# A fused attention and expert kernel: the row scores run six steps ahead of the column scores instead of eight

## The chip, the cores and the metric

The kernel runs on one core of one Trainium2 chip. The metric is the device time of one execution in microseconds (us). A TensorE clock of 1.00 in the profile is the full 2.4 GHz, 0.50 is 1.2 GHz. Engines are named as the profile names them: PE is TensorE, DVE is VectorE, ACT is ScalarE, POOL is GpSimd, SP is SyncE, which issues most DMAs here.

## The reference, cut to what matters

```
x: 16 batches x 512 tokens x 256 features, 16 heads of 16
n = layernorm(x)
Q, K, V = n Wq^T + bq, n Wk^T + bk, n Wv^T + bv          (per head)
scores  = Q K^T / 4 + lambda * (tanh(Q) J) tanh(K)^T      (causal: j > i gives -inf)
x = x + softmax(scores) V Wo^T + bo
x = x + swiglu_shared(layernorm(x)) + sum over the top 2 of 8 experts, each weighted
```

The change touches only the attention stage, which is a little over half of the time. The routing and the experts after it are the same before and after.

## The kernel before, in words

Attention works on one batch at a time, in 16 steps of one batch (`STEPS`). Four groups of four heads make four steps each: step n handles head group n // 4 and the key tile jt = n % 4 of 128 keys. Because of the causal mask, the scores of that step are (4 - jt) * 128 wide: 512, 384, 256, 128 columns in the four steps of a group.

Each score is computed twice. The **columns** (keys on the partitions, queries along the free axis, `ps_cols`, L532 and L536) are what the softmax uses. ACT takes their exponential (L623), POOL zeroes the masked corner (L801), and PE multiplies with V (`pv`, L554) one step later. The exponential must have each row's maximum taken off. The maximum comes from the **rows** (queries on the partitions, `ps_rows`, L525), which PE computes LEAD steps ahead: DVE adds the mask and takes the maximum in one instruction per head (L680, followed by a short read of the accumulator into `mx`). When the four row tiles of a head group are done, DVE writes the negated maxima as two parts into `nm` (L689, L691). PE turns them with four transposes into `ps_m` (the piece `"mt"`, L463), ACT copies them to `mT` (L610), and the matmul of L536 adds them to the columns. The first columns of a group wait for this copy.

A step is made of two halves, s = 0 and s = 1. In a half PE issues two heads of rows and the two other heads of columns, four matmuls side by side in the array, and then L536 for these columns. There are three PSUM banks for rows and three for columns. So a half can be issued only when DVE has finished the first maximum of the half before, and ACT the first exponential of the half before. After half 0 comes the "piece" with place 0, after half 1 `pv` of the step before and the piece with place 1. In `PIECES` an entry is (step, place, kind, index, batch relative to the one whose columns run). Pieces are the projections and the other small products: `xt` transposes of the normalized input, `k`, `q`, `qj`, `v` projections of the next batch, `mt` turned maxima, `out` output projection, `gt` and `lg` the router's part of the batch before. All pieces use one PSUM bank, `ps_m`, and each waits until the engine that empties it has taken the piece before (`taken`).

DVE's order in a step is: maxima of half 0, its part of piece 0, maxima of half 1 and, at the end of a head group, the two instructions on `nm`, then piece 1. After that follow, at some steps, small jobs: `invert` (n = 1 and 9), `normalize` (L731, n = 5 and 13), `layer_norm` of the input of the batch after next (L667, n = 9), `statistics` (n = 11 to 14).

With LEAD = 8 and tiles numbered from the widest down, the rows of step n are just as wide as its columns, and a group of rows begins at a step with n % 4 = 0 and ends at n % 4 = 3. Before batch 0 there is a prologue of 16 steps without columns: the projections of batch 0, then, from step 8 on, eight steps of rows alone, with six banks (`first_rows`), among which DVE takes the statistics of the later inputs (L755). In the last batch the rows end at step 7, and eight steps of columns alone follow.

The k and q data go through SP's DMAs into `ks` and `qs`, and the first rows of a batch (step 8 of the batch before) wait for them. All instructions are unrolled; there is no loop register.

Of the kernel before, what the change touches and what calls it, by code (L numbers as in the profile page):

```python
# [34 lines left out]
TT = S // P  # L35
NT = NB * TT
HG = 4
# [7 lines left out]
NSLOT = 2 * NT + NE - 1  # L45
ZR = 3
EARLY = 4
LEAD = 8
STEPS = G * TT
STRIP = 2 * HD  # L50
PART_PAIRS = ((0, 0), (0, 1), (1, 0))
# [29 lines left out]
def over_batches(eng, batch):  # L81
# [7 lines left out]

PIECES = [  # L90
    (0, 0, "xt", 0, 1), (0, 1, "xt", 1, 1),
    (1, 0, "mt", 1, 0),
    (2, 0, "k", 0, 1),
    (3, 0, "k", 1, 1),
    (4, 0, "q", 0, 1),
    (5, 0, "q", 1, 1), (5, 1, "mt", 2, 0),
    (6, 0, "qj", 0, 1),
    (7, 0, "qj", 1, 1),
    (8, 0, "v", 0, 1),
    (9, 0, "v", 1, 1), (9, 1, "mt", 3, 0),  # L100
    (10, 0, "out", 0, -1),
    (11, 0, "out", 1, -1),
    (12, 0, "gt", 0, -1),
    (13, 0, "gt", 1, -1),
    (14, 0, "mt", 0, 1),
    (15, 0, "lg", 0, -1),
]
PER_BATCH = {"xt": 2, "k": 2, "q": 2, "qj": 2, "v": 2, "mt": G, "out": 2, "gt": 2, "lg": 1}
# [67 lines left out]
def attention_stage(nc, ctx, sbt, x_v, wqT, bq, wkT, bk, wvT, bv, woT, bo, J, lam,  # L176
# [213 lines left out]
    def count(kind, j, b):  # L390

        return b.v * PER_BATCH[kind] + j + 1

    def unit(b, n):

        m = n + LEAD
        return b.plus(m // STEPS), (m % STEPS) // TT, TT - 1 - m % TT

    def row_no(g, it, h):

        return (g * TT + TT - 1 - it) * HG + h

    def col_no(n, s, e):

        return n * HG + 2 * s + e

    def bank_of(u):

        return 1 if u == STEPS * HG - 1 else u % 3

    def first_rows(d, u):

        return d.off == 0 and u < STEPS * HG // 2

    def row_bank(d, u):

        return (*ps_rows, *ps_cols)[u % 6] if first_rows(d, u) else ps_rows[bank_of(u)]

    def last_use(u):

        w = u - 1
        while bank_of(w % (STEPS * HG)) != bank_of(u):
            w -= 1
        return w
# [4 lines left out]
    def _(pe):  # L429
# [55 lines left out]
        def half(b, n, s):  # L485

            HEADS = STEPS * HG
            d, g, it = unit(b, n)
            gc, jt = n // TT, n % TT
            has_rows = d.at_least(0) and d.at_most(NB - 1)  # L490
            has_cols = b.at_least(0) and b.at_most(NB - 1)
            if has_rows and first_rows(d, row_no(g, it, 0)):
                if s == 1:
                    return
                if g == 0 and it == TT - 1:
                    for loaded in (k_in, q_in):
                        pe.wait_ge(loaded[0], 64)
                if row_no(g, it, 3) >= 6:
                    pe.wait_ge(max_done, row_no(g, it, 3) - 5)
                for h in range(HG):  # L500
                    at = STRIP * h
                    mm = nc.tensor.matmul(row_bank(d, row_no(g, it, h))[:, 0:(it + 1) * P],
                                          qs[at:at + STRIP, d.par, g, it * P:(it + 1) * P],
                                          ks[at:at + STRIP, d.par, g, 0:(it + 1) * P], start=True, stop=True)
                    if h % 2:
                        mm.then_inc(rows_ready, 1)
                return
            if has_rows:
                if g % 2 == 0 and it == TT - 1 and s == 0:
                    for loaded in (k_in, q_in):  # L510
                        pe.wait_ge(loaded[g // 2], (d.v + 1) * 64)
                w = max(last_use(row_no(g, it, 2 * s + e)) for e in range(2))
                if w >= 0 or d.at_least(1):
                    pe.wait_ge(max_done, d.v * HEADS + w + 1)
            if has_cols:
                if s == 0 and jt == 0:
                    pe.wait_ge(taken["mt"], count("mt", gc, b))
                w = max(last_use(col_no(n, s, e)) for e in range(2))
                if w >= 0 or b.at_least(1):
                    pe.wait_ge(exp_done, b.v * HEADS + w + 1)  # L520
            if has_rows:
                for e in range(2):
                    h = 2 * s + e
                    at = STRIP * h
                    mm = nc.tensor.matmul(ps_rows[bank_of(row_no(g, it, h))][:, 0:(it + 1) * P],  # L525
                                          qs[at:at + STRIP, d.par, g, it * P:(it + 1) * P],
                                          ks[at:at + STRIP, d.par, g, 0:(it + 1) * P], start=True, stop=True)
                mm.then_inc(rows_ready, 1)
            if has_cols:
                for e in range(2):  # L530
                    at = STRIP * (2 * (1 - s) + e)
                    nc.tensor.matmul(ps_cols[bank_of(col_no(n, s, e))][:, jt * P:S], ks[at:at + STRIP, b.par, gc, jt * P:(jt + 1) * P],  # L532
                                     qs[at:at + STRIP, b.par, gc, jt * P:S], start=True, stop=False)
                for e in range(2):
                    at = STRIP * (2 * (1 - s) + e)
                    mm = nc.tensor.matmul(ps_cols[bank_of(col_no(n, s, e))][:, jt * P:S], ones_r[at:at + STRIP],  # L536
                                          mT[at:at + STRIP, gc % 2, jt * P:S], start=False, stop=True)
                mm.then_inc(cols_ready, 1)
# [19 lines left out]
        def batch(b):  # L558
            att = b.at_least(0) and b.at_most(NB - 1)
            for n in range(STEPS):  # L560
                if b.fixed and b.off == PROLOGUE and n == 8:
                    pe.wait_ge(const_ready, 2)
                half(b, n, 0)
                piece(b, n, 0)
                half(b, n, 1)
                if n > 0 and att:
                    pv(b, n - 1)
                if n == 0 and b.at_least(1):
                    pv(b.plus(-1), STEPS - 1)
                if b.off == TAIL and n == 0:  # L570
                    pe.wait_ge(max_done, NB * STEPS * HG)
                    fill(ps_rows[0], 42)
                if b.off == TAIL and 10 <= n < 15:
                    fill(ps_rows[0], 3)
                piece(b, n, 1)
# [81 lines left out]
    def _(dve):  # L657
# [12 lines left out]
        def maximum(b, n, s):  # L670
            d, g, it = unit(b, n)
            if not (d.at_least(0) and d.at_most(NB - 1)):
                return
            gb = g % 2
            dve.wait_ge(rows_ready, d.v * (STEPS * 2) + row_no(g, it, 2 * s) // 2 + 1)
            dve.nop(nofuse=True)
            for e in range(2):
                h = 2 * s + e
                bank = row_bank(d, row_no(g, it, h))[:, 0:(it + 1) * P]
                nc.vector.tensor_tensor_reduce(out=bank, in0=bank, in1=maskrow[:, (TT - 1 - it) * P:S], scale=1.0,  # L680
                                               scalar=LOWEST, op0=ALU.add, op1=ALU.max, accum_out=mx[:, gb, it, h:h + 1])\
                    .then_inc(max_done, 1)
            if it == 0 and s == 1:

                dve.wait_ge(max_done, d.v * (STEPS * HG) + (g + 1) * TT * HG)
                if g > 0 or d.at_least(1):
                    dve.wait_ge(ready["mt"], d.v * G + g)
                pair = nm[:].rearrange("p t (h c) -> p t h c", c=STRIP)
                nc.vector.tensor_scalar(pair[:, :, :, 0], mx[:, gb], -1.0, None, ALU.mult).then_inc(nmh_ready, 1)  # L689
                dve.wait_ge(nmh_ready, d.v * G + g + 1)  # L690
                nc.vector.scalar_tensor_tensor(out=pair[:, :, :, 1], in0=mx[:, gb], scalar=-1.0,  # L691
                                               in1=pair[:, :, :, 0].bitcast(F32), op0=ALU.mult, op1=ALU.subtract)\
                    .then_inc(nm_ready, 1)
# [1135 lines left out]
```

## Time and profile before

| | |
|---|---|
| time, median of 3 runs | 2139.71 us (2135.65 to 2140.8) |
| profiled execution, its own time | 2137.79 us |
| its span, first to last instruction | 2136.1 us |
| PE, DVE, ACT, POOL busy | 92%, 58%, 50%, 38% of the span |
| prologue, rows alone | 57.99 to 87.19 us |
| batches with columns | 87.19 to 1147 us |

A timeline row of the profile gives the start in us, the duration in us, the engine, the source line, the operation, output and inputs, and how many instructions were merged; in brackets stands how long the engine was idle before and what ended that.

### The profile page before, as it was taken

How to read it: one execution, taken by the hardware profiler on the slowest of the kernel's cores; microseconds unless marked ns; L12 is line 12 of the kernel's file. 1: busy time of each engine (PE TensorE's matmuls, PEld its weight loads, DVE VectorE, ACT ScalarE, POOL GpSimd, SP SyncE). 2: the span in 40 equal slices, each digit the busy share in tenths (PEclk: the TensorE clock that was granted, in tenths of full speed). 3: DMA queues.
4: the chain of work that ended last, by engine and by line, in shares of the span. 5: the costliest groups of instructions: out<-in, count | busy, mean ns of one | idle time of the engine just before them, and what ended most of it. 6: DMA issues, size and time to landing. Idle time of an engine off the chain costs nothing. (4 is left out here: it accounts for less than half of the span.)

```text
span 2136.1 us, 48445 instructions
## 1 busy us (share of the span) xinstructions
PE 1957.2 (92%) x14755; PEld 1296.5 (61%) x14824; DVE 1246.5 (58%) x3875; ACT 1065.7 (50%) x2310; POOL 820.6 (38%) x1206
## 2 busy tenths in 40 slices
PE   2689999999999999999988999997999999999997
PEld 1345445454454544545435788886777777777776
DVE  5666667766667666776662865553445545444553
ACT  1255555555555555555552345452555555555553
POOL 4033323333323333233332037773444444444443
PEclk9799999999999999999999999999999999999999
DMA  7234443344443434434322346654863333333332
GB/s 240 60 106 117 121 136 124 110 118 119 136 130 107 122 111 140 128 114 124 100 87 79 137 134 226 223 188 150 215 167 58 57 55 55 56 55 57 54 57 34
DMA packets 156641, 246.08 MB, mean 115 GB/s; under 512 B 29408, under 2 KB 90592, under 8 KB 156480
## 3 DMA queue, kind: packets, MB, share of 16 engines
q1 hardware_dynamic: 120960, 189.24, 28.9%
q0 software_dynamic: 32064, 53.44, 12.2%
q8 instruction: 91, 1.49, 0.3%
q10 hardware_dynamic: 3456, 1.34, 0.3%
q14 instruction: 70, 0.57, 0.1%
HBM read 111.89 MB, written 90.50 MB: 95 GB/s over the span
## 5 line engine op out<-in xcount | busy, mean ns | idle before, releaser
L680 DVE CUSTOM_DVE_ANT_0 ps_rows<-ps_rows,maskrow 128x128 f32<-128x128 f32 (+1 forms) x1009 | 477.1, 514 | 290.9 <-PE ps_rows L525 282.2
L623 ACT ACTIVATE probs<-ps_cols 128x512 f32<-128x512 f32 (+3 forms) x1024 | 392.0, 435 | 386.7 <-PE ps_cols L536 380.1
L525 PE MATMUL ps_rows<-ks,qs 32*128 32x512 f32 x1984 | 403.1, 480 | 73.5 <-DVE mx L680 38.6
L532 PE MATMUL ps_cols<-qs,ks 32*128 32x512 f32 (+3 forms) x2048 | 418.5, 485 | 2.5 <-ACT probs L623 2.4
L1642 POOL DMA_INDIRECT out_dram<-y_e,to x135 | 216.1, 1601 | 349.4 <-DMA out_dram<-y_e,to 221.5
L799 POOL TENSOR_TENSOR pace<-eps 1x1 f32<-1x1 f32 x256 | 58.2, 227 | 747.0 <-ACT probs L623 747.0
L525 PEld LDWEIGHTS ps_rows<-ks,qs 32*128 32x128 f32 x1984 | 153.3, 184 | 268.5 <-DVE mx L680 221.9
L536 PE MATMUL ps_cols<-mT,ones_r 32*128 32x512 f32 (+3 forms) x1024 | 284.8, 550 | 0.0
L1771 DVE TENSOR_TENSOR h_lo<-ps_h,h_hi 128x512 fp32r<-128x512 f32 x135 | 93.3, 691 | 232.6 <-ACT h_hi L1746 232.6
L1740 ACT ACTIVATE sg_e<-ps_ge 128x512 f32<-128x512 f32 x135 | 80.7, 598 | 263.1 <-PE ps_ge L1664 261.0
L554 PE MATMUL ps_o<-probs,vt 128*32 128x512 f32 (+3 forms) x2048 | 192.5, 448 | 0.8 <-POOL probs L801 0.8
L1407 POOL DMA_INDIRECT xs_d<-row,pos x128 | 131.3, 1026 | 134.2 <-issue 118.5
L532 PEld LDWEIGHTS ps_cols<-qs,ks 32*128 32x128 f32 x2048 | 154.8, 185 | 9.7 <-ACT probs L623 7.6
L801 POOL TENSOR_SCALAR_AFFINE_SELECT probs<-probs 128x512 f32<-128x512 f32 x256 | 159.8, 624 | 0.0
L680 DVE DVE_READ_ACCUMULATOR2_ANT mx<- 128x1 f32 x1024 | 144.4, 141 | 0.1
L1787 DVE TENSOR_TENSOR h_e<-sg_e,ps_ue 128x512 f32<-128x512 f32 x135 | 92.9, 688 | 71.1 <-PE ps_ue L1664 71.1
L1633 POOL DMA_DIRECT2D xr<-xs_d x133 | 127.6, 959 | 14.8 <-DVE to L1796 14.1
L536 PEld LDWEIGHTS ps_cols<-mT,ones_r 32*128 32x128 f32 x1024 | 99.5, 188 | 51.3 <-issue 31.5
L1664 PE MATMUL ps_ge<-w_hi,x_lo 128*128 x270 | 111.4, 493 | 0.0
L1664 PE MATMUL ps_ue<-w_hi,x_lo 128*128 x270 | 109.2, 485 | 0.0
L1080 PE MATMUL ps_g<-x2T,swg 128*128 128x512 f32 x384 | 99.8, 396 | 1.4 <-DVE x2T L1190 1.4
L1133 ACT ACTIVATE sg<-ps_g 128x512 f32<-128x512 f32 x64 | 37.9, 593 | 126.6 <-PE ps_g L1080 94.6
(220 smaller groups left out, 3838.9 us busy)
## 6 DMA issues: line engine op xcount, KB each, us to landing
xs_d<-zrows SPq DMA_DIRECT2D x45, 408.0 KB, 2.9
xr<-xs_d POOLq DMA_DIRECT2D x135, 136.0 KB, 3.3
whi_d<-w_sh SPq DMA_DIRECT2D x16, 768.0 KB, 3.8
w_hi<-whi_d SPq DMA_DIRECT2D x24, 512.0 KB
xn<-in_L_attn_x_dram SPq DMA_DIRECT2D x16, 512.0 KB, 5.2
ks<-k_lin SPq DMA_DIRECT2D x64, 128.0 KB, 3.0
ks<-k_tan SPq DMA_DIRECT2D x64, 128.0 KB, 3.7
qs<-q_lin SPq DMA_DIRECT2D x64, 128.0 KB, 2.4
```

Source lines behind the costliest of these rows:

```text
L525: mm = nc.tensor.matmul(ps_rows[bank_of(row_no(g, it, h))][:, 0:(it + 1) * P], qs[at:at + STRIP, d.par, g, it * P:(it + 1) * P], ks[at:at ...
L532: nc.tensor.matmul(ps_cols[bank_of(col_no(n, s, e))][:, jt * P:S], ks[at:at + STRIP, b.par, gc, jt * P:(jt + 1) * P], qs[at:at + STRIP, b. ...
L536: mm = nc.tensor.matmul(ps_cols[bank_of(col_no(n, s, e))][:, jt * P:S], ones_r[at:at + STRIP], mT[at:at + STRIP, gc % 2, jt * P:S], start= ...
L554: mm = nc.tensor.matmul(ps_o[2 * HD * h:2 * HD * (h + 1), jt * P:S], vt[:, b.par, jt, g * HG + h], probs[:, n % 2, h, jt * P:S], start=jt ...
L623: nc.scalar.activation(probs[:, n % 2, 2 * (1 - s) + e, jt * P:S], ps_cols[bank_of(col_no(n, s, e))][:, jt * P:S], ACT.Exp).then_inc(exp_d ...
L680: nc.vector.tensor_tensor_reduce(out=bank, in0=bank, in1=maskrow[:, (TT - 1 - it) * P:S], scale=1.0, scalar=LOWEST, op0=ALU.add, op1=ALU.m ...
L801: nc.gpsimd.affine_select(out=blk, in_=blk, compare_op=ALU.is_ge, fill=0.0, base=0, pattern=[[0, HG], [1, P]], channel_multiplier=-1).then ...
L1080: mm = nc.tensor.matmul(bank[i % 2][:], w[:, wp, k, i * P:(i + 1) * P], self.x2T[:, s.par, xp, k], start=at == 0 and k == 0, stop=at == 2 ...
L1407: nc.gpsimd.indirect_dma_start(xs_d[:, :], bass.IndirectOffsetOnAxis(ap=pos[:, t, r:r + 1], axis=0), row[q][:, r], None).then_inc(scattere ...
L1633: pool.dma_start(xr[:, s.par], rows_of(xs_v, s.plus(2))).then_inc(x_loaded[s.par], 16)
L1642: nc.gpsimd.indirect_dma_start(out_v, bass.IndirectOffsetOnAxis(ap=to[:, d.quad], axis=0), y[:, d.par], None, bounds_check=NT * P - 1, oob ...
L1664: mm = nc.tensor.matmul(bank, part[:, k], w[side][:, k * width:(k + 1) * width], start=at == 0 and k == 0, stop=at == 2 and k == n - 1)
```

## The change

LEAD becomes 6. The tile of rows in step n is still the one as wide as the step's columns, so the rows of a head group now come in the order 256, 128, 512, 384 (function `turn_of` gives a tile's place in that order), and a group begins at n % 4 = 2 and ends at n % 4 = 1. DVE's two instructions on `nm` move with the end of the group. The four `mt` pieces move: from (step 1, place 0), (5, 1), (9, 1) and (14, 0) to (2, 1), (6, 1), (10, 1) and (14, 1). The rows before batch 0 take six steps of the prologue, 10 to 15, and in the last batch the rows end at step 9. The wait for the k and q data moves with the first rows of groups 0 and 2.

```diff
-LEAD = 8
+LEAD = 6
...
-    (1, 0, "mt", 1, 0),
-    (2, 0, "k", 0, 1),
+    (2, 0, "k", 0, 1), (2, 1, "mt", 1, 0),
     (3, 0, "k", 1, 1),
     (4, 0, "q", 0, 1),
-    (5, 0, "q", 1, 1), (5, 1, "mt", 2, 0),
-    (6, 0, "qj", 0, 1),
+    (5, 0, "q", 1, 1),
+    (6, 0, "qj", 0, 1), (6, 1, "mt", 2, 0),
...
-    (9, 0, "v", 1, 1), (9, 1, "mt", 3, 0),
-    (10, 0, "out", 0, -1),
+    (9, 0, "v", 1, 1),
+    (10, 0, "out", 0, -1), (10, 1, "mt", 3, 0),
...
-    (14, 0, "mt", 0, 1),
+    (14, 1, "mt", 0, 1),
...
         m = n + LEAD
-        return b.plus(m // STEPS), (m % STEPS) // TT, TT - 1 - m % TT
+        return b.plus(m // STEPS), (m % STEPS) // TT, TT - 1 - n % TT
+
+    def turn_of(it):
+
+        return (TT - 1 - it + LEAD) % TT
 
     def row_no(g, it, h):
 
-        return (g * TT + TT - 1 - it) * HG + h
+        return (g * TT + turn_of(it)) * HG + h
...
-        return d.off == 0 and u < STEPS * HG // 2
+        return d.off == 0 and u < LEAD * HG
...
-                if g == 0 and it == TT - 1:
+                if g == 0 and turn_of(it) == 0:
...
-                if g % 2 == 0 and it == TT - 1 and s == 0:
+                if g % 2 == 0 and turn_of(it) == 0 and s == 0:
...
-            if it == 0 and s == 1:
+            if turn_of(it) == TT - 1 and s == 1:
```

## Rows read from the trace of the kernel before

**Rows 1.** Windows view, batch 6: busy PE, PEld, DVE, ACT, POOL; clock.

```profile
486.90:553.25 66.35, 61.34 (x565) 32.67 (x565) 44.99 (x164) 36.83 (x86) 21.73 (x46) 1.00 0.41 122
```

**Rows 2.** Source view of L525: what ended idle time before it (us, times).

```profile
  DVE mx L680: 260.5, 447
```

**Rows 3.** Timeline of the prologue, PE, then DVE.

```profile
57.99 1.23 PE L502 MATMUL ps_rows<-ks,qs 32*128 32x512 f32 x3 [2.85 <-DMA qs<-q_mix]
...
60.02 2.93 PE L458 MATMUL ps_m<-wvp,xT 128*128 128x256 f32 x12
...
87.19 1.22 PE L525 MATMUL ps_rows<-ks,qs 32*128 32x512 f32 x2 [1.25 <-DVE mx L680]
...
70.56 1.40 DVE L755 BATCH_NORM_STATS2 st<-probs 128x6 f32<-128x256 f32 x4
...
78.35 0.70 DVE L680 CUSTOM_DVE_ANT_0 ps_cols<-ps_cols,maskrow 128x512 f32<-128x512 f32 x1 [1.35 <-PE ps_rows L502]
...
84.20 0.43 DVE L680 CUSTOM_DVE_ANT_0 ps_rows<-ps_rows,maskrow 128x256 f32<-128x256 f32 x1 [0.41 <-PE ps_cols L502]
```

**Rows 4.** Timeline of batch 6, step 1: DVE's maximum and PE's turning.

```profile
493.17 0.56 DVE L680 CUSTOM_DVE_ANT_0 ps_rows<-ps_rows,maskrow 128x384 f32<-128x384 f32 x1
...
493.31 0.66 PE L463 MATMUL ps_m<-ident,nm 128*128 128x128 f32 x4 [0.88 <-DVE xT L699]
```

**Rows 5.** Timeline of batch 6, steps 2 and 3, PE.

```profile
499.03 0.85 PE L554 MATMUL ps_o<-probs,vt 128*32 128x384 f32 x8
500.27 0.38 PE L525 MATMUL ps_rows<-ks,qs 32*128 32x128 f32 x2 [0.39 <-ACT probs L623]
...
500.77 1.66 PE L446 MATMUL ps_m<-xT,wkp 128*128 128x512 f32 x6
```

**Rows 6.** Source views, L689 and L691: duration ns min/median/max; first, last start.

```profile
L689 DVE TENSOR_SCALAR nm<-mx x64: 181/619/1004, 76.6 to 1112.0; 128x16 fp32r<-128x16 f32 x64
...
L691 DVE SCALAR_TENSOR_TENSOR nm<-mx,nm x64: 186/189/700, 76.8 to 1112.7; 128x16 fp32r<-128x16 f32 x64
```

**Rows 7.** Timeline of batch 6, steps 5, 6 and 8.

```profile
514.00 0.66 PE L463 MATMUL ps_m<-ident,nm 128*128 128x128 f32 x4
...
514.70 0.60 ACT L610 ACTIVATE mT<-ps_m 128x512 fp32r<-128x512 f32 x1 [0.37 <-PE ps_m L463]
...
516.41 0.48 PE L525 MATMUL ps_rows<-ks,qs 32*128 32x256 f32 x2
...
520.97 0.70 PE L525 MATMUL ps_rows<-ks,qs 32*128 32x512 f32 x2 [0.33 <-issue]
...
514.04 0.69 DVE L731 TENSOR_TENSOR onT<-o_val,o_inv 128x512 f32<-128x512 f32 x1
```

**Rows 8.** Timeline of batch 6, steps 9 and 10.

```profile
534.00 0.49 PE L525 MATMUL ps_rows<-ks,qs 32*128 32x256 f32 x2
...
531.04 2.48 DVE L667 TENSOR_SCALAR xn<-xn,mv,rstd 128x256 f32<-128x256 f32 x4
533.43 0.42 DVE L680 CUSTOM_DVE_ANT_0 ps_rows<-ps_rows,maskrow 128x256 f32<-128x256 f32 x1
```

**Rows 9.** Timeline of batch 6, step 12, PE.

```profile
541.53 0.70 PE L525 MATMUL ps_rows<-ks,qs 32*128 32x512 f32 x2 [0.48 <-DVE mx L680]
```

**Rows 10.** Timeline of batch 6, steps 14 and 15.

```profile
548.98 0.48 PE L525 MATMUL ps_rows<-ks,qs 32*128 32x256 f32 x2
...
552.03 0.38 PE L525 MATMUL ps_rows<-ks,qs 32*128 32x128 f32 x2 [0.36 <-DVE mx L680]
...
548.46 0.41 DVE L680 CUSTOM_DVE_ANT_0 ps_rows<-ps_rows,maskrow 128x256 f32<-128x256 f32 x1
```

**Rows 11.** The last batch: timeline of PE, steps 9 and 11.

```profile
1115.92 1.65 PE L532 MATMUL ps_cols<-qs,ks 32*128 32x384 f32 x4 [0.34 <-ACT probs L623]
...
1130.36 0.49 PE L532 MATMUL ps_cols<-qs,ks 32*128 32x128 f32 x4
```

**Rows 12.** Windows view, last batch, columns as in rows 1.

```profile
1116.00:1118.00 2.00, 1.89 (x6) 0.76 (x6) 0.00 (x0) 0.92 (x3) 1.48 (x4) 0.50 0.00 0
```

## The prediction

> **What bounds the kernel now.** I read the page first, then the timeline of the prologue, of one ordinary batch and of the last one, then windows for the clock, and last the source lines that the change moves. The reader should see three things. First, the ordinary batches are one repeated schedule: batch 6 runs from its first rows matmul to the next batch's in 66.35 us at a granted clock of 1.00, with PE busy 61.34 us and DVE only 44.99 us [rows 1]. A microsecond gained or lost in it is gained or lost 15 or 16 times. Second, PE is busy nearly all the time but not free of waits: before the rows matmuls it sat idle 260.5 us in 447 places until DVE had a maximum done [rows 2] (weight loads included, so partly hidden behind matmuls). A half waits for the first maximum of the half before. So what counts is where DVE does its other jobs, and whether a piece on PE covers that. Third, the ends: a prologue of rows alone from 57.99 to 87.19 us, started by the landing of q_mix [rows 3], and a last batch in which the clock falls to 0.50 for a while [rows 11, 12].
>
> **The matmuls.** Widths stay paired, rows as wide as columns in every step, and no matmul, maximum or exponential is added or taken away. A middle batch keeps its work; only the order changes. The changed step arithmetic is done before the run and costs nothing.
>
> **Prologue.** Rows start at step 10 instead of 8. Both v projections, in steps 8 and 9, now come before them. They need not wait for q_mix, whose last piece is done about 2 us before the rows start now, so the first goes at about 56 us. At the low clock such a piece takes 2.93 us [rows 3], plus some 0.8 us until DVE has taken it, so the second ends at about 62.6. The rows start there, 4.6 us later than now. What follows is shorter. One 512 and one 384 step go: the two after the first turning last from 77.00 (78.35 less 1.35 idle) to 83.79 (84.20 less 0.41), 6.8 us [rows 3]. One `nm` pair goes, 0.55 us (below). One of DVE's statistics jobs (1.40 us and its closing, 1.7 us) and the two v copies (my estimate 1.5 us together) move ahead into PE's 4.6 us. So 29.2 - 6.8 - 0.55 - 1.7 - 1.5 = 18.6 us, and batch 0 starts at 62.6 + 18.6 = 81.2 instead of 87.19: -6 us, between -3 (nothing moves ahead) and -8 (the clock is high in the v pieces).
>
> **Step 1.** The turning there waits 0.88 us for DVE's `xT` [rows 4], and one would book a gain of 15 waits. I book none. DVE's next maximum waits for the same `xT`: it starts at 493.17, and its 0.56 us with the accumulator read end at about 493.85, which is also when the turning ends (0.59 us from 493.31). Both release the same half.
>
> **Steps 2 to 4.** The turning goes behind `pv` of step 2. That ends near 499.85, while the next half starts only at 500.27, held by ACT [rows 5]. The turning takes 0.59 us of PE (in step 5 it starts at 514.00 and the next half at 514.59), ACT's copy starts 0.70 us after its start and takes 0.60 us [rows 7]. So the half starts at 500.45, but the k piece, which needs `ps_m` empty, at about 499.85 + 1.35 = 501.2 instead of 500.77 [rows 5]. ACT hands that on. +0.4 us, between +0.2 and +0.7.
>
> **What the `nm` pair costs DVE.** The two instructions take 0.18 and 0.19 us at their shortest, with the waits on the semaphore between and before about 0.55 us; at their median and longest the first takes 0.62 and 1.00 us, the second 0.19 and 0.70 [rows 6]. The long ones lie beside POOL's work. In the new places (steps 1, 5, 9, 13) the pair follows a 384-wide maximum, and POOL's mask starts at the same time behind the last exponential, so I take 1.2 us, with 0.55 and 1.7 as the bounds. Before, the pair stood at steps 3, 7 and 15, where it delayed nothing, and at step 11. Rule: the Trainium skill, SBUF — State Buffer, Who interferes with whom, says that GpSimd and a VectorE tensor_scalar in its two-port mode, or a VectorE instruction with two SBUF inputs, take the shared ports for whole instructions, the later one blocking. By it both of the pair can block in turn, 1.7 us, and the sum below would come to 2196 us instead of 2180.
>
> **Steps 5 to 8.** The turning leaves step 5 (-0.59) and comes back in step 6 (+0.59). Between them stands DVE: after the maximum of step 5 it does the pair and then `normalize`, 0.69 us from 514.04 [rows 7]. With 1.2 us more the next maximum is ready at about 516.4, the next half starts there instead of at 516.41, and the early start is lost. Then +0.59 for the turning, and in step 7 the next piece waits 0.3 us for ACT's copy, since a 128-wide half is shorter (0.5 us) than the copy's 1.35. Against it, the wait of 0.33 us before step 8 [rows 7] may go: I read it as the landing of q_mix, now needed two steps later. +0.3, between -0.1 and +0.7.
>
> **Steps 9 to 11.** The same, with a longer job behind the pair: `layer_norm`, 2.48 us from 531.04, slowed by POOL, and the next maximum at 533.43 releases the half at 534.00 [rows 8]. A pair before it moves that by 0.4 (it uses up POOL's busy time, and `layer_norm` runs faster) to 1.2. Then +0.59 for the turning and +0.25 for the wait on its copy. +1.3, between +0.9 and +1.9. Queued behind on DVE stands the `out` addition, which the turning's bank waits for; it still ends in time.
>
> **Step 12.** The pair is gone from its front; the half that waits 0.48 us for DVE [rows 9] comes earlier. -0.35.
>
> **Steps 13 to 15.** After the maxima of step 13 DVE does the pair, `normalize` and a statistics instruction. The next maximum is already a little late at 548.46, and 0.52 us later, at 548.98, PE's half follows [rows 10]. Here the piece that covered it is also gone. +1.2 for the pair, +0.59 for the turning, now at place 1. Of this the later wait in step 15 (0.36 us before 552.03 [rows 10]) gives something back, and the router's piece waits for the copy of `mT`: +1.65 net, between +0.9 and +2.0.
>
> **Sum.** 0.4 + 0.3 + 1.3 - 0.35 + 1.65 = +3.3 us a batch, between +1.9 and +4.9 by all bounds at once. In 15 batches (0 to 14) that is 49 us. The last batch has no k, q, v pieces and no turning at step 14; some 1 us more. Its slow clock: steps 9 and 10 take 14.44 us, from 1115.92 to 1130.36 [rows 11], where PE works at 0.50 [rows 12]. I estimate 5.8 us of that as the clock's price (PE works through, at half the speed, for some 13 us, part of it covered). With rows in steps 8 and 9 it may come or not; I take -0.5. Total 2137.8 - 6 + 49 + 1 - 0.5 = 2181 us against the profiled execution's 2137.79. The median of the runs shown is 2139.71, 1.9 us above, so between 2181 and 2183 for a median; I say 2181.
>
> **Rivals.**
> A, *only the turnings cost* (12%): the pair is hidden, by running 0.55 us beside POOL and in DVE's slack (it is busy 44.99 of 66.35 us [rows 1]). Then 0.4 - 0.1 + 0.85 - 0.35 + 0.45 = +1.25 a batch, 19 - 6 = +13: 2151 us. Against it: DVE's other jobs stand right behind the pair in three of the four new places.
> B, *faster* (8%): DVE's backlog and the turnings are all covered, and the wait of 0.33 us before step 8 [rows 7] goes: -6 - 15 x 0.3 = -10.5, 2127 to 2129 us. It decides as soon as the batch takes less than 66.35 us [rows 1]. Against it: PE's `pv`, turning and half follow one another without a gap at 514.00 and 514.59 [rows 7], so a turning at place 1 is not free.
> C, *the clock* (6%): PE's new waits, above all over 1 us in step 14, could bring the low clock into every batch. A stretch like that of the last batch costs 5.8 us; 15 of them on top of the forecast give 2268 us. For it: the fall in the last batch came after waits of 0.3 to 0.7 us in a row. Against it: 61.34 us of 66.35 busy would become about 61 of 70. The Trainium skill, TensorE: Matmul & The Clock Gate, A second HAM failure mode: psum-queue depth-cycling, names small idles between groups of matmuls from cycling banks as a cause of a swinging clock. By that rule this rival would come; the trace shows it only where the rows had ended.
> D, *no change* (6%): two or three of the small delays don't come and the rest pays for the prologue, +0.4 a batch: 2138 us.
>
> **Numbers.** The forecast with 68%, its own range 2158 to 2205. The range 2150 to 2204 takes in A and leaves out B, C and D. A measurement of this kernel tells about 0.3%, 6.4 us. Faster 0.08 (B), same 0.06 (D), slower 0.86.
>
> **What the profile would show.** Batch period near 69.6 us in the middle batches; first half of columns at about 81 us; step 14's half 0 lasting about 2.7 us instead of 1.5 (548.98 less 547.48 by the start of the half before); the `nm` instructions longer than before, with a median above 0.6 us; no wait on DMA at step 10; clock 1.00 in the middle. The prediction is wrong if the period stays within 0.5 us of 66.35, which means that DVE's jobs had cover that I didn't see, or if the clock falls in the middle batches.

## The result: 50 us slower, most of it in the middle batches

The changed kernel takes 2190.78 us (median of 4 runs, 2184.09 to 2193.47); beside it the kernel before took 2140.26. The ratio is 1.0228, 95% interval 1.0208 to 1.0248. The forecast was 2181 us with a range of 2150 to 2204. The profiled execution has a span of 2186.9 us, 50.8 more than before.

The windows view of the kernel after, for the batch that stands in the place of [rows 1], and for one that is longer:

```profile
core 0: us, PE busy (x) PEld busy (x) DVE busy (x) ACT busy (x) POOL busy (x), PEclk, DMA share, GB/s
507.23:576.39 69.16, 61.69 (x564) 32.67 (x565) 44.73 (x164) 36.56 (x86) 21.53 (x46) 1.00 0.39 114
364.12:435.97 71.85, 64.64 (x568) 34.16 (x564) 44.63 (x163) 36.63 (x86) 21.51 (x46) 0.95 0.38 113
```

No engine has more work in the first than before (PE 61.34, DVE 44.99 us [rows 1]). The batch is 2.8 us longer in waits alone. The second has PE busy 3 us longer, at a granted clock of 0.95: part of it ran at half speed. So there are two losses. The starts of the batches in the timeline separate them from each other and from the two ends (us; both columns are of the profiled execution):

| part | before | after | difference |
|---|---|---|---|
| start to first columns | 87.19 | 83.57 | -3.6 |
| batches 0 to 14 | 997.40 | 1052.33 | +54.9 |
| of these, 15 times the undisturbed batch | 66.35 each | 69.16 each | +42.1 |
| the rest, nearly all of it the clock | | | +12.8 |
| last batch to the start of its last `pv` | 62.85 | 61.81 | -1.0 |
| all that follows | 988.7 | 989.2 | +0.5 |

The undisturbed batch, step by step, as medians over the batches at full clock (a step from its first rows matmul to the next step's):

| steps | before | after | difference | forecast |
|---|---|---|---|---|
| 0, 1 | 9.02 | 8.97 | -0.05 | 0 |
| 2 to 4 | 13.45 | 13.84 | +0.4 | +0.4 |
| 5 to 8 | 16.68 | 16.92 | +0.25 | +0.3 |
| 9 to 11 | 13.05 | 14.22 | +1.2 | +1.3 |
| 12 | 4.59 | 4.31 | -0.3 | -0.35 |
| 13 to 15 | 9.58 | 10.93 | +1.35 | +1.65 |

The last batch is 1.0 us shorter, against +0.5 in the forecast (+1 of work, -0.5 of clock): the fall of the clock in its steps 9 and 10, 13.6 us long before, did not come, and one of 3.4 us came in step 6.

How such a loss looks in the trace: the timeline of the kernel after around step 14, which answers to [rows 10]. L692 and L694 are the `nm` pair, L734 is `normalize`, L528 the rows matmul, L466 the turning, L484 the router's piece.

```profile
849.74 0.48 PE L528 MATMUL ps_rows<-ks,qs 32*128 32x256 f32 x2
849.94 0.62 POOL L804 TENSOR_SCALAR_AFFINE_SELECT probs<-probs 128x512 f32<-128x512 f32 x1
849.95 0.66 DVE L692 TENSOR_SCALAR nm<-mx 128x16 fp32r<-128x16 f32 x1
...
850.64 0.19 DVE L694 SCALAR_TENSOR_TENSOR nm<-mx,nm 128x16 fp32r<-128x16 f32 x1
850.74 0.69 DVE L734 TENSOR_TENSOR onT<-o_val,o_inv 128x512 f32<-128x512 f32 x1
851.35 0.42 DVE L740 BATCH_NORM_STATS2 st<-xres 128x6 f32<-128x256 f32 x1
851.68 0.41 DVE L683 CUSTOM_DVE_ANT_0 ps_rows<-ps_rows,maskrow 128x256 f32<-128x256 f32 x1
...
852.21 0.48 PE L528 MATMUL ps_rows<-ks,qs 32*128 32x256 f32 x2 [1.64 <-DVE mx L683]
...
853.75 0.66 PE L466 MATMUL ps_m<-ident,nm 128*128 128x128 f32 x4
...
854.34 0.38 PE L528 MATMUL ps_rows<-ks,qs 32*128 32x128 f32 x2
...
855.10 0.64 PE L484 MATMUL ps_m<-x1T,gwp 128*32 128x128 f32 x16 [0.19 <-ACT mT L613]
```

The rows of 849.74 are in the bank by about 850.6, but DVE comes to them at 851.68, behind pair, `normalize` and statistics. PE stands 1.64 us. The 16-element instruction takes 0.66 us, as long as POOL's mask beside it, against 0.18 at its shortest [rows 6]. From one half to the next are 2.47 us where there were 1.50. Then comes the turning, now without cover, and the router's piece waits for its copy.

Step 9 shows the same with a longer job behind the pair, and one thing that I had counted on: `layer_norm` (L670) takes 1.54 us instead of 2.48 [rows 8], since the pair has used up POOL's busy time. In the kernel before POOL is busy beside these four instructions for 1.64 us, here for 0.42; where POOL is idle they take 1.38.

```profile
551.82 0.62 POOL L804 TENSOR_SCALAR_AFFINE_SELECT probs<-probs 128x512 f32<-128x512 f32 x1
551.84 0.99 DVE L692 TENSOR_SCALAR nm<-mx 128x16 fp32r<-128x16 f32 x1
552.06 0.48 PE L528 MATMUL ps_rows<-ks,qs 32*128 32x256 f32 x2 [0.37 <-DVE mx L683]
552.40 0.39 POOL L816 CAST w_sh<-w_st 128x256 fp32r<-128x256 f32 x1
552.87 0.19 DVE L694 SCALAR_TENSOR_TENSOR nm<-mx,nm 128x16 fp32r<-128x16 f32 x1
...
553.23 1.54 DVE L670 TENSOR_SCALAR xn<-xn,mv,rstd 128x256 f32<-128x256 f32 x4
554.69 0.42 DVE L683 CUSTOM_DVE_ANT_0 ps_rows<-ps_rows,maskrow 128x256 f32<-128x256 f32 x1
555.22 0.48 PE L528 MATMUL ps_rows<-ks,qs 32*128 32x256 f32 x2 [0.40 <-DVE mx L683]
```

And the clock, in windows of two microseconds around step 15 of batch 4. The last columns are granted clock, DMA share and GB/s.

```profile
428.00:430.00 2.00, 0.40 (x10) 0.38 (x10) 1.89 (x7) 0.66 (x2) 0.00 (x0) 1.00 0.97 338
430.00:432.00 2.00, 2.00 (x22) 1.00 (x14) 1.51 (x10) 0.66 (x2) 0.77 (x2) 0.75 0.21 71
432.00:434.00 2.00, 2.00 (x28) 1.33 (x26) 0.85 (x7) 1.04 (x3) 0.00 (x0) 0.50 0.29 93
434.00:436.00 2.00, 2.00 (x26) 0.96 (x22) 0.90 (x5) 0.45 (x2) 0.40 (x2) 0.50 0.48 170
436.00:438.00 2.00, 2.00 (x14) 0.83 (x10) 0.00 (x0) 0.00 (x0) 0.36 (x1) 0.54 0.00 0
438.00:440.00 2.00, 1.80 (x20) 0.95 (x14) 1.51 (x5) 1.57 (x3) 0.00 (x0) 1.00 0.00 0
```

PE has 0.40 us of work in the two microseconds of step 14's wait. Just after, the clock falls to 0.50. Eight of the batches 1 to 14 are longer by 1.2 to 2.7 us in this way, nearly all of it in steps 14, 15 and 0; a stretch at 0.50 lasts 3.3 to 6.8 us and begins in each of the eight in the second half of step 14. Five take 69.16 or 69.17 us, and batch 14, which has no `layer_norm`, 68.69.

### The profile page after: what moved, and what is told of

The parts are those of the page before. It is cut to its first block and busy times, and to the rows that moved or that the text cites. A ratio compares the mean times of both kernels' runs of the same rounds, so it can differ in the third digit from the quotient of the medians.

```text
span 2186.9 us, 48516 instructions
## 1 busy us (share of the span) xinstructions
PE 1979.6 (91%) x14823; PEld 1304.3 (60%) x14824; DVE 1245.0 (57%) x3875; ACT 1063.2 (49%) x2310; POOL 818.6 (37%) x1206
## 5 line engine op out<-in xcount | busy, mean ns | idle before, releaser
L683 DVE CUSTOM_DVE_ANT_0 ps_rows<-ps_rows,maskrow 128x384 f32<-128x384 f32 (+1 forms) x1012 | 478.9, 514 | 346.1 <-PE ps_rows L528 342.4
L528 PE MATMUL ps_rows<-ks,qs 32*128 32x512 f32 x2000 | 413.9, 488 | 114.8 <-DVE mx L683 91.4
L802 POOL TENSOR_TENSOR pace<-eps 1x1 f32<-1x1 f32 x256 | 47.0, 184 | 801.6 <-ACT probs L626 801.6
L528 PEld LDWEIGHTS ps_rows<-ks,qs 32*128 32x128 f32 x2000 | 157.8, 187 | 313.2 <-DVE mx L683 253.5
L1636 POOL DMA_DIRECT2D xr<-xs_d x133 | 118.0, 887 | 14.8 <-DVE to L1799 13.9
L1097 PE MATMUL ps_y<-swd,hT 128*128 128x256 f32 x768 | 97.4, 287 | 2.2 <-DVE hT L1184 2.2
```

The costliest lines, as they stand in the source:

```text
L1636: pool.dma_start(xr[:, s.par], rows_of(xs_v, s.plus(2))).then_inc(x_loaded[s.par], 16)
```

## The experiments

All ran against the kernel before on the same chip, which took medians of 2139.05 to 2140.65 us in the three groups. Batch times are those of undisturbed middle batches, from their windows.

### The turnings alone

`lead8_late_turnings` leaves LEAD at 8 and the pair at steps 3, 7, 11, 15, and takes only the new places of the pieces:

```diff
-    (1, 0, "mt", 1, 0),
-    (2, 0, "k", 0, 1),
+    (2, 0, "k", 0, 1), (2, 1, "mt", 1, 0),
...
-    (5, 0, "q", 1, 1), (5, 1, "mt", 2, 0),
-    (6, 0, "qj", 0, 1),
+    (5, 0, "q", 1, 1),
+    (6, 0, "qj", 0, 1), (6, 1, "mt", 2, 0),
...
-    (9, 0, "v", 1, 1), (9, 1, "mt", 3, 0),
-    (10, 0, "out", 0, -1),
+    (9, 0, "v", 1, 1),
+    (10, 0, "out", 0, -1), (10, 1, "mt", 3, 0),
...
-    (14, 0, "mt", 0, 1),
+    (14, 1, "mt", 0, 1),
```

> The kernel before (LEAD 8, the nm pair at steps 3, 7, 11, 15) with only the four mt pieces at the places of the kernel after: (2,1), (6,1), (10,1), (14,1). My account: the turnings alone cost 0.4 us in steps 2 to 4, 0.85 in 9 to 11, 0.45 in 13 to 15 and about nothing in 5 to 8, so a batch takes 66.35 + 1.7 = 68.05 us and the kernel 2166 us. Rival, that only the pair in front of DVE's other jobs costs: batch 66.35, 2140 us. Rival, that the turnings carry the whole loss: batch 69.2 or more, 2180 to 2191 us.

2168.21 us, ratio 1.0118 (1.0101 to 1.0136). The batch:

```profile
568.91:637.18 68.27, 61.64 (x565) 32.63 (x565) 44.47 (x164) 36.55 (x86) 22.10 (x46) 1.00 0.39 119
```

The turnings alone cost 1.9 of the 2.8 us: 0.4 in steps 2 to 4, 0.35 in 5 to 8, 0.8 in 9 to 11, 0.4 in 13 to 15. Both rivals are out. My account has it but for steps 5 to 8, where I had expected that the wait before step 8 takes up the 0.3 us of step 7; it stayed at 0.33 to 0.37 us. The 0.9 us that are left for the pair are the difference of two kernels. No run has the pair in its new places with the turnings in the old ones.

In steps 9 to 11 the turning uncovers a job of DVE. The second half of step 9 becomes 0.59 us shorter without it, but the next half 0.54 us longer (3.23 us instead of 2.69), because `layer_norm` stands in front of its maxima.

### DVE's other jobs moved from behind the pair

```diff
-                    if n == 5:
+                    if n == 6:
                         normalize(b.plus(-1), 1)
...
-                    if n == 13:
+                    if n == 15:
                         normalize(b, 0)
...
-                if n == 9 and b.plus(2).at_most(NB - 1):
+                if n == 10 and b.plus(2).at_most(NB - 1):
                     layer_norm(b.plus(2))
```

> The kernel after, with three of DVE's jobs taken from behind the nm pair: normalize of the batch before from step 5 to 6, layer_norm from 9 to 10, normalize of the batch itself from 13 to 15. Turnings and pair stay. My account: it takes 0.5 us out of step 6, 0.8 out of step 10 and 0.6 out of step 14, some 1.9 us a batch, so an undisturbed batch takes 67.3 us; with fewer falls of the clock 2150 us, with as many 2162 us. Rival, that the pair alone delays DVE, not what stands behind it: less than 0.5 us a batch, 2184 us or more. Rival, turnings only: no change, 2191 us.

2150.14 us, ratio 1.0043 (1.0021 to 1.0065): 41 us less than the changed kernel, with LEAD 6, the pair and the turnings left where they are.

The batch in the windows view, then step 14 in the timeline:

```profile
483.74:551.54 67.80, 61.54 (x564) 32.67 (x565) 44.58 (x165) 36.55 (x86) 22.04 (x46) 1.00 0.39 119
```
```profile
545.22 0.66 DVE L692 TENSOR_SCALAR nm<-mx 128x16 fp32r<-128x16 f32 x1
...
546.35 0.42 DVE L683 CUSTOM_DVE_ANT_0 ps_rows<-ps_rows,maskrow 128x256 f32<-128x256 f32 x1
...
546.88 0.48 PE L528 MATMUL ps_rows<-ks,qs 32*128 32x256 f32 x2 [1.03 <-DVE mx L683]
```

Without `normalize` the wait is 1.03 us, not 1.64. The batch is 1.4 us shorter, against 1.9 expected (0.3 in step 6, 0.5 in step 10, 0.6 in step 14), and the clock fell in only one of the batches 1 to 14, in step 1 and not in step 14.

The first columns came at 78.05 us, 5.5 earlier than in the kernel after, and that is not the edit's doing. From the first rows to the first columns both kernels took 18.8 us, but the rows started at 59.29 us instead of 64.81. The clock differed, as the windows of the prologue show, first the kernel after, then this one:

```profile
48.00:64.00 16.00, 12.03 (x31) 7.52 (x32) 4.65 (x23) 3.96 (x6) 0.00 (x0) 0.50 0.91 260
```
```profile
48.00:64.00 16.00, 8.41 (x50) 5.24 (x50) 8.81 (x39) 4.08 (x6) 0.00 (x0) 1.00 0.82 250
```

With the same edit and the banks counted on (`lead6_jobs_regular`, below) the rows started at 64.17 us again. So the total met its number partly by luck: the batches gained 0.5 us less each than expected, and the prologue's clock gave 5.5 us.

### The clock: fills in step 14

```diff
                 piece(b, n, 0)
+                if n == 14 and b.at_least(1) and b.at_most(NB - 2):
+                    pe.wait_ge(taken["gt"], count("gt", 1, b.plus(-1)))
+                    fill(ps_m, 5)
                 half(b, n, 1)
```

> The kernel after, with five filling matmuls of 512 columns into ps_m on PE in step 14 behind half 0 of batches 1 to 14; their result is overwritten. PE waits 1.64 us for DVE there, and 5 such matmuls take about 1.1 us at the full clock. If that wait lets the granted clock fall, the falls in the middle batches go and every batch takes 69.16 us, the kernel 2178 us (13 less). If the falls have another cause, or cost nothing that counts, it stays at 2191 us, and if the fills lie on the path, 15 x 0.5 or more above.

2179.1 us, ratio 1.0172 (1.0148 to 1.0195), 12 us less than the changed kernel. Of the batches 1 to 14, ten took 69.15 to 69.17 us, one 69.47 and one 68.68 at full clock. Two (70.75 and 70.80) still had a low stretch of 3.4 us, about step 1.

```profile
503.49:572.65 69.16, 63.05 (x570) 33.53 (x570) 44.73 (x164) 36.55 (x86) 21.49 (x46) 1.00 0.39 116
```

PE is busy 1.4 us longer, the batch is the same to the hundredth, and the falls behind step 14 are gone. They are gone too in `lead6_jobs_later`, which has no fills but a shorter wait there (1.03 us). So it is shown that the wait in step 14 brings them, and the 12 us are their price. The two low stretches about step 1 begin right behind another wait, of 1.41 us, which the moved turning leaves in step 1 (the kernel before waits 0.88 us there [rows 4]).

All falls of the clock in batches 1 to 14 of the twelve profiled executions lie right behind such a wait. Behind the 1.64 us of step 14 it fell in 8 of 14 batches, behind the 1.41 us of step 1 in 5 of 70 (five kernels), and behind waits of 1.02 us in step 13 of `lead7` and `lead7_regular_banks` in 2 of 28. Behind 1.03 us in step 14 (`lead6_jobs_later`, `lead6_jobs_regular`) and 1.22 in step 9 (`lead7`) it did not fall, nor in the five kernels whose longest wait in these batches is 0.89 us or less.

### LEAD 7

A group of rows then ends at n % 4 = 0, the pair stands at steps 0, 4, 8, 12, and the turnings have their old places.

```diff
-LEAD = 6
+LEAD = 7
...
-        return d.off == 0 and u < LEAD * HG
+        return d.off == 0 and u < 24
```

> The kernel after with LEAD 7: rows 512, 384, 256, 128 beside columns of the same widths, groups of rows end at n % 4 = 0, so the nm pair stands at steps 0, 4, 8 and 12, one step ahead of DVE's jobs, and the turnings stand at the places of the kernel before. The prologue has seven steps of rows, the last with three banks. My account: pair and turnings are covered but for 0.3 to 0.6 us in step 13, against which 0.35 us of step 12 and up to 0.3 us of wait before step 8 go; a batch takes 66.2 to 66.6 us, the prologue is 2 to 3 us shorter: 2134 to 2140 us. Rival, that a shorter lead costs in itself, in waits for maxima or for k and q data: a batch of 67.5 us or more, 2155 us or more.

2147.22 us, ratio 1.0032 (1.0022 to 1.0043): missed. The batch takes 67.39 us, and the timeline of step 8 shows where:

```profile
521.51 0.70 PE L529 MATMUL ps_rows<-ks,qs 32*128 32x512 f32 x2
...
522.79 0.70 DVE L684 CUSTOM_DVE_ANT_0 ps_rows<-ps_rows,maskrow 128x512 f32<-128x512 f32 x1 [0.42 <-PE ps_rows L529]
...
523.41 0.73 DVE L684 CUSTOM_DVE_ANT_0 ps_rows<-ps_rows,maskrow 128x512 f32<-128x512 f32 x1
...
524.46 0.59 PE L529 MATMUL ps_rows<-ks,qs 32*128 32x384 f32 x2 [1.22 <-DVE mx L684]
```

PE does not go on after the first maximum (about 523.6) but after the second. The code says why: `bank_of` puts head number 63, the last of a batch, in bank 1 in place of 0, so that the next batch can begin with bank 0. The half behind it needs bank 1 and waits for head 63, the second of its pair. With LEAD 8 this falls behind a 128-wide half, with LEAD 7 behind a 512-wide one, with LEAD 6 behind the 384-wide one of step 9. I had not seen it in the prediction. The other part is step 13, whose first half takes 2.71 us: the pair, then statistics, in front of its maxima. The prologue had an error the other way: the first columns came at 80.98 us, 6.2 earlier than in the kernel before, where I had expected 2 to 3.

### The banks counted on

```diff
-    def bank_of(u):
+    def bank_of(d, u):
 
-        return 1 if u == STEPS * HG - 1 else u % 3
+        return (d.off * STEPS * HG + u) % 3
```

with `last_use(u)` now u - 3.

> LEAD 7 with the banks counted on. In the LEAD 7 run a batch took 67.40 us, 1.0 more than before; step 8's second half had 2.95 us instead of 2.15 and step 13's first half 2.71 instead of 1.78. If the first of these is the exception of head 63, which LEAD 7 puts behind a 512-wide half, it falls to 2.15, a batch takes 66.5 us, and the kernel 2147 - 15 x 0.9 = 2133 us. If it is the lead itself, nothing changes: 2147 us.

2136.78 us, ratio 0.9988 (0.9969 to 1.0006). The half of step 8 falls from 2.95 to 2.30 us, where 2.15 was expected, so the exception was worth 0.65 us. The time is 3.8 us above the 2133 expected. The batch:

```profile
413.05:479.64 66.59, 61.23 (x568) 32.60 (x564) 45.29 (x164) 36.90 (x86) 21.78 (x45) 1.00 0.41 122
```

> The kernel before, with the score banks counted on through all batches (head number modulo 3) in place of the exception that puts the last head of a batch, number 63, in bank 1. With the exception the half behind that head waits for the second maximum of the half before, not the first. Two readings of the wait of 0.33 us before step 8. If it is this exception, step 7's second half falls from 1.47 to about 1.07 us, the half before step 0 (columns' exception) by some 0.15, a batch takes 65.8 us and the kernel 2132 us. If it is the landing of the k and q data, as I wrote in the prediction, step 7 stays and the batch takes 66.2 us, 2138 us.

2137.28 us, ratio 0.9986 (0.9973 to 0.9999). The batch takes 66.12 us; step 7's second half falls from 1.47 to 1.25 us (1.21 to 1.30), not to 1.07, and the half before step 0 stays at 1.22.

The windows view of the batch, and the timeline of the two halves:

```profile
486.45:552.57 66.12, 61.34 (x564) 32.64 (x565) 44.96 (x164) 36.84 (x86) 21.75 (x46) 1.00 0.40 122
```
```profile
519.05 0.38 PE L522 MATMUL ps_rows<-ks,qs 32*128 32x128 f32 x2
...
520.30 0.70 PE L522 MATMUL ps_rows<-ks,qs 32*128 32x512 f32 x2
```

So the wait before step 8 had two causes one behind the other, neither of my readings alone: 0.2 us of bank exception, and 0.15 to 0.2 behind it. With LEAD 7 and 6 the half takes 1.06 us.

The second is not the landing of q_mix. In the prologue, where PE does wait for it, the rows start 0.14 us after the landing of the last part that they need. In `lead8_regular_banks` this part had landed 0.35 to 0.74 us before the rows of step 8. In `lead8_late_turnings` it had landed 1.0 to 1.8 us before, and the half took the same 1.47 us as in the kernel before. And the half before step 0, where the rows of head group 2 begin, is as much longer (1.22 us, against 1.06 in `lead7_regular_banks` and `lead6_jobs_regular`), though their data landed some 30 us earlier.

What the places have in common is that the first rows of groups 0 and 2 have two more waits in PE's program, for `k_in` and `q_in`. With LEAD 7 these stand before step 9, and the half in front of them is the one that takes 2.30 us instead of 2.15. With LEAD 6 they stand before step 10, and there they cost nothing (2.03 us). No run takes them out, so this cause is not shown.

> lead6_jobs_later (a batch of 67.81 us, 2150 us) with the banks counted on. By the same account the half before step 10 falls from 2.47 to 2.03 us and the one before step 0 by 0.15: a batch of 67.2 us, 2141 us. What is left against the kernel before, 0.9 us a batch, would be the turnings behind half 1 and the pair in step 13. If the exception is not what holds the half before step 10, 2150 us.

2141.43 us, ratio 1.0007 (0.9992 to 1.0023), as expected; step 9's second half takes 2.03 us instead of 2.47.

```profile
350.62:417.90 67.28, 61.46 (x568) 32.62 (x564) 44.45 (x164) 36.55 (x86) 22.06 (x45) 1.00 0.41 120
```

So a lead of six steps can be had at the time of the kernel before, once the banks and DVE's jobs move with it. The batch is still 0.9 us longer than before. In the profiled executions the batches 0 to 14 take 12.5 us more together, and the prologue (first columns at 82.94 us) and the last batch 4.2 us less each. Against the kernel with a lead of eight and the same banks the batch is 1.15 us longer.

### Fills in the last batch, and the best version

In `half`, where only columns are left:

```diff
+            if has_cols and not has_rows and jt < 3 and n + s > STEPS - LEAD:
+                pe.wait_ge(max_done, NB * HEADS)
+                fill(ps_rows[0], 2 if jt == 0 and s == 1 else 1)
```

> As lead8_regular_banks, and in the last batch, where only columns are left, one or two filling matmuls of 512 columns into a free rows bank before the halves that wait for ACT. If the waits there let the clock fall, the fall in steps 9 and 10 goes and gives back about 5 us: 2127 us. If the fall has another cause, the fills only cost their own time, up to 2 us: 2134 us.

2131.3 us, ratio 0.996 (0.9941 to 0.998). Windows of 14 us in the last batch, first without the fills (`lead8_regular_banks`), where the clock was low, then with them:

```profile
1112.00:1126.00 14.00, 13.16 (x54) 6.77 (x52) 0.97 (x2) 4.58 (x10) 3.67 (x8) 0.51 0.04 12
```
```profile
1112.00:1126.00 14.00, 13.73 (x96) 6.87 (x96) 3.49 (x11) 6.66 (x17) 6.59 (x11) 1.00 0.04 13
```

The last batch, up to the start of its last half, falls from 60.5 to 56.5 us. In steps 8 to 10 the fills give back 5.3 us, near the 5.8 that the prediction had put on the low clock, and in steps 11 to 13, where no clock was low, they cost 1.35 us. The fall does not need fills to stay away: with LEAD 7 and the banks counted on, the profiled execution had none in steps 8 to 10. In the profiled execution with the fills the clock was low for some 17 us in batch 0 (72.09 us instead of 68), which the fills do not touch.

The last two add one edit: the statistics of steps 11 and 12 both go to step 10, behind whose maxima the `out` matmuls cover DVE.

```diff
-                if 11 <= n < 11 + TT and piece_exists(b, -1):
-                    statistics(b.plus(-1), n - 11)
+                if piece_exists(b, -1):
+                    for t in {10: (0, 1), 13: (2,), 14: (3,)}.get(n, ()):
+                        statistics(b.plus(-1), t)
```

> lead8_regular_fill, and the two statistics instructions of steps 11 and 12 both at step 10, where out's matmuls cover DVE. By my account of the pair's place, step 12 was late because pair and statistics stood in front of its maxima: 2.44 us falls to 2.15, a batch takes 65.8 us, the kernel 2126 us. If the statistics do not hold the half, 2131 us.

2130.73 us, ratio 0.9957 (0.9942 to 0.9972). Step 12 falls from 4.59 to 4.31 us as expected and the batch to 65.85; the time is above the 2126 expected and cannot be told from `lead8_regular_fill`'s.

```profile
485.56:551.41 65.85, 61.35 (x564) 32.67 (x565) 44.89 (x164) 36.83 (x86) 21.73 (x46) 1.00 0.41 123
```

> lead7_regular_banks with the same two additions (statistics of steps 11 and 12 at step 10, fills in the last batch). The pair now stands alone in front of step 13: its first half falls from 2.71 to about 2.35 us, a batch takes 66.25 us, the kernel 2131 us. If what delays step 13 is the pair alone, 2136 us.

2133.5 us, ratio 0.9973 (0.9957 to 0.9988). Step 13's first half takes 2.41 us, the batch 66.3, as expected; the time is 2.5 us above the 2131 expected. Batch 0 took 72.99 us, 20 of them at half clock, in the profiled execution.

Both are faster than the kernel before by more than their intervals, by 0.3 to 0.4%. Which of the two is faster is open.

## Why the prediction was right, point by point

**The mechanism.** Right. The loss sits in the batch, which does the same work in more time, and comes from the places of the pair and of the turnings. Met among its signs were the batch (69.16 us, forecast 69.6), step 14's first half (2.47 us, forecast 2.7), and no wait on a DMA at step 10. `nm`'s median of 0.66 us tells little, as it was 0.62 before. Missed were the first half of columns (83.57 us, forecast 81) and the clock.

**One of its own signs of being wrong came.** It had named "if the clock falls in the middle batches", and the clock fell in eight of them. So the mechanism is right for the 42 us and lacks the 12 us of the clock.

**Its sums.** The low end of the range by all bounds at once is +1.55 us a batch by the terms given (0.2 - 0.1 + 0.9 - 0.35 + 0.9), not +1.9. The term of steps 5 to 8 comes by its own parts to +0.56 us (-0.59 + 0.59 + 0.59 + 0.3 - 0.33), and +0.3 was taken.

**Step 1, booked at nothing.** Right: -0.05 us, although the wait of [rows 4] is gone there. DVE's maximum waits for the same `xT`.

**Steps 2 to 4, 9 to 11 and 12.** Right within 0.15 us.

**Steps 5 to 8.** The number taken is right within 0.1 us, two parts are not. The early start (-0.50) was only half lost again in step 6 (+0.27), where all of it had been booked as lost. The turning cost its 0.59 us and the wait on its copy 0.26. The half before step 8 gave back 0.41 us (1.47 to 1.06), but not because q_mix came in time, as I had read it: 0.2 us of it were the bank exception, and the rest is open.

**Steps 13 to 15.** The term was too large, +1.65 against +1.35. The pair took 0.66 and 0.19 us there, about 1.0 with its waits instead of 1.2, and step 15 gave more back. Of the two instructions only the first was held by POOL, for up to 1.01 us in all; the second took 0.20 us at most in the 64 places of the kernel after. So the 1.7 us of both together came nowhere.

**What I did not see.** The exception in `bank_of`. It is worth 0.44 us in step 9's second half. Here it changed little, because the next half waited for DVE anyway: fixed together with the jobs it was worth 0.5 us a batch (67.80 to 67.28), and it decided the LEAD 7 run.

**The prologue.** Mis-sized: -3.6 instead of -6. The rows started at 64.81 us, not at 62.6. The two `qj` pieces before them ran at half clock (2.07 us each), the first v piece began at 58.20 instead of 56, and the second ended at 64.8. From there to the first columns took 18.8 us; I had 18.6. What was mis-sized is the clock before the rows, and it differs between executions: with the same LEAD of 6 the rows started at 59.29, 64.17, 64.81 and 65.82 us.

**The clock.** I had given it 6% as "in every batch" and 87 us. In the profiled execution it came in eight of fourteen batches, and it cost 12 us, as the fills show. This is the missing part of the forecast: 2181 from a batch term of 49 us that measures 42, and no term for the clock, which measures 12. With the prologue (2.4 us too low) and the last batch (1.5 too high) this gives the 7 us between the forecast and the profiled execution. The misses are of opposite sign, and that the total came so near is partly luck. As an all-or-nothing rival the clock was put wrongly; it should have been a term of its own with its chance per batch. The Trainium skill, TensorE: Matmul & The Clock Gate, A second HAM failure mode: psum-queue depth-cycling, names small idles between groups of matmuls from cycling banks; here one wait of 1.64 us in step 14 did it, and the many of up to 0.88 us in the kernel before brought no fall in its batches 1 to 14.

**Rival A, only the turnings.** Wrong as a whole, but the turnings are two thirds of the batch's loss, 1.9 us, more than its 1.25. The pair adds the other third. **B and D** are out.

## What to carry to other kernels

When work is reordered inside a repeated schedule, write down for each moved instruction what stands behind it on its engine and what stood beside it as cover. Here a pair of instructions that takes 0.4 us alone, put in front of `normalize` and `layer_norm`, and four turnings moved out of a covered place, cost 42 us in 15 batches. Moving DVE's other jobs one or two steps away gives back half. If two buffers rotate with an exception at the wrap, look at which step the exception falls; a change of lead moves it. And where a new long wait appears in front of matmuls, give the clock a term of its own beside the wait.

## What the runs showed of the hardware

Five matmuls of 512 columns put in front of a wait of 1.64 us kept the granted clock at 1.00 behind step 14 in all middle batches, at no cost to the batch (69.16 us with and without). One or two before a half of columns did so in the last batch, where they gave back 5.3 us and cost 1.35.

A VectorE instruction on 16 elements a partition took 0.18 us where POOL was idle, 0.66 beside POOL's mask of 0.62, and 0.99 where POOL's cast of 0.39 followed the mask. Four `layer_norm` instructions took 1.38 us where POOL was idle, 1.54 with POOL busy for 0.42 us beside them, and 2.48 with 1.64 us.

Rows that waited for the landing of a DMA, in the prologue of eight kernels, started 0.14 us after it.

In batches 1 to 14 the granted clock fell only right behind the longest waits of PE: behind 1.64 us in 8 of 14 batches, behind 1.41 us in 5 of 70, behind 1.02 us in 2 of 28.
